# Layer 0's score maxima: two 64-row products per head pair instead of one product against a masked key operand

## What is computed

```
x = x + tanh(g_xattn[0]) * L0_xattn(layernorm(x), ctx)      # 16 heads of 64, 120 keys
x = x + tanh(g_ffn[0])   * L0_ffn(layernorm(x))             # 8 experts, weighted
x = x + tanh(g_xattn[1]) * L1_xattn(layernorm(x), ctx)      # 16 heads of 16, 120 keys
x = x + tanh(g_ffn[1])   * L1_ffn(layernorm(x))             # first 512 tokens

def L0_xattn(x, context):
    q, k, v = heads of x @ Wq.T, context @ Wk.T, context @ Wv.T
    sim = einsum('bihd,bjhd->bhij', q, k) * 64 ** -0.5
    attn = softmax(sim)                       # over the 120 keys
    return (attn @ v) @ Wo.T + bo
```

## Time and profile before

| | before |
|---|---|
| median of three runs | 3786.83 us (3785.24 to 3787.05) |
| the profiled execution's own time, its span | 3787.4 us |
| PE busy | 3715.2 us, 98% of the span |
| PE weight loads (PEld) busy | 2972.8 us, 78% |
| DVE busy | 2656.0 us, 70% |
| ScalarE (ACT) busy | 1751.9 us, 46% |
| POOL busy | 1382.3 us, 36% |
| one turn of the main loop | 56.50 us (layer 1's key product starts at 1800.51 us, the next batch's at 1857.01) |

### The profile page before, as it was taken

How to read it: one execution, slowest core, us unless ns; L and a number is a source line. 1 busy time by engine, 2 the same in 40 slices (tenths; PEclk the granted TensorE clock), 3 DMA queues, 4 the chain that set the end, 5 groups by cost and what they waited for, 6 DMA issues and landing times.

```text
span 3787.4 us, 96515 instructions
## 1 busy us (share of the span) xinstructions
PE 3715.2 (98%) x34836; PEld 2972.8 (78%) x34836; DVE 2656.0 (70%) x5694; ACT 1751.9 (46%) x3371; POOL 1382.3 (36%) x1333
## 2 busy tenths in 40 slices
PE   6999999999999999999999999999999999999998
PEld 5788788788788788878878878878878878878865
DVE  4676776776776776776776776777777777677675
ACT  4444445444445445445445445445444444444431
POOL 3334334334334334334334333333333333333323
PEclk9999999999999999999999999999999999999999
DMA  3000000000000000000000000000000000000011
GB/s 95 10 15 11 16 14 11 16 15 11 15 16 9 15 16 9 15 16 9 15 16 9 15 16 9 15 16 10 14 16 14 11 16 14 11 16 14 11 37 53
DMA packets 58915, 64.81 MB, mean 17 GB/s; under 512 B 5344, under 2 KB 55808, under 8 KB 58240
## 3 DMA queue, kind: packets, MB, share of 16 engines
q10 hardware_dynamic: 34688, 32.52, 2.8%
q1 hardware_dynamic: 24192, 31.81, 2.5%
HBM read 47.01 MB, written 17.30 MB: 17 GB/s over the span
## 4 chain that ended last, share of the span: by engine, by line
PE 84%; DVE 10%; issue 2%; POOL 1%; DVEq 1%; ACT 0%; POOLq 0%
PE g L821 25%; PE g L827 15%; PE scores L821 10%; PE scores L923 6%; PE g L981 6%; DVE xn L1179 4%; PE g L890 4%; PE g L990 3%; PE scores L974 3%; DVE y_nm L1257 3%; PE scores L955 3%; PE g L841 3%; PE scores L927 2%; PE g L901 1%; POOL y_rstd L543 1%
## 5 line engine op out<-in xcount | busy, mean ns | idle before, releaser
L760 ACT ACTIVATE prob<-scores 120x1024 f32<-120x1024 f32 x512 | 510.2, 1023 | 495.6 <-PE scores L927 324.5
L1318 DVE SCALAR_TENSOR_TENSOR x<-g,lg_w,x 128x256 f32<-128x256 f32 x1024 | 483.5, 482 | 59.6 <-PE g L821 32.2
L596 POOL TENSOR_TENSOR q_lo<-an,q_hi 128x512 fp32r<-128x512 f32 x256 | 329.5, 1287 | 345.0 <-ACT q_hi L793 345.0
L662 ACT CAST q_hi<-g 128x512 fp32r<-128x512 f32 x256 | 150.1, 586 | 579.1 <-PE g L821 579.1
L821 PE MATMUL g<-ew_hi,yT_hi 128*128 128x512 f32 x1024 | 412.0, 402 | 0.0
L541 POOL TENSOR_TENSOR y_rstd<-y_mv,eps 128x2 f32<-128x2 f32 x128 | 25.0, 195 | 1041.5 <-DVE y_mv L1174 1041.5
L821 PE MATMUL g<-ew_lo,yT_hi 128*128 128x512 f32 x1024 | 401.2, 392 | 0.0
L821 PE MATMUL g<-ew_hi,yT_lo 128*128 128x512 f32 x1024 | 399.7, 390 | 0.0
L1257 DVE TENSOR_REDUCE x_nm<-g 128x4 f32<-128x480 f32 x512 | 310.6, 649 | 104.8 <-PE g L890 104.8
L1257 DVE TENSOR_REDUCE y_nm<-g 128x4 f32<-128x480 f32 x512 | 301.1, 651 | 109.7 <-PE g L901 109.7
L591 POOL TENSOR_TENSOR q_lo<-q_full,q_hi 128x512 fp32r<-128x512 f32 x256 | 328.6, 1303 | 38.3 <-ACT q_full L694 38.0
(11 more groups left out here) (213 smaller groups left out, 9905.8 us busy)
## 6 DMA issues: line engine op xcount, KB each, us to landing
x_in<-in_x ACTq DMA_DIRECT2D x64, 256.0 KB, 2.9
out<-y_x SPq DMA_DIRECT2D x64, 256.0 KB, 2.1
ctx_in<-in_ctx ACTq DMA_DIRECT2D x128, 120.0 KB, 2.5
wk_s<-in_gu SPq DMA_DIRECT2D x8, 512.0 KB, 3.6
vx<-in_ew SPq DMA_DIRECT2D x2, 1024.0 KB, 5.1
wk_s<-in_wk SPq DMA_DIRECT2D x1, 1024.0 KB, 5.1
prob<-in_wq SPq DMA_DIRECT2D x1, 1024.0 KB, 7.8
wv_s<-in_wv SPq DMA_DIRECT2D x1, 1024.0 KB, 10.4
```

The costliest lines, as they stand in the source:

```text
L596: g.tensor_tensor(q[1][:, 2 * h:2 * h + 2, :], an[:, 2 * (h % 2):2 * (h % 2) + 2, :], q[0][:, 2 * h:2 * h + 2, :].bitcast(F32), ALU.subtra ...
L662: a.copy(dst, ring.bank(job)[:, 0:cols]).then_inc(done.sem, 1)
L760: a.activation(prob[:, e % 2].rearrange("p o u s -> p (o u s)"), scores[0:NK, banks, :].rearrange("p o c -> p (o c)"), ACT.Exp, scale=scal ...
L1318: ins = v.scalar_tensor_tensor(out=x1[:, t, :], in0=ring.bank(Y_FFN[j])[:, o * D:(o + 1) * D], scalar=lg_w[:, t, 2 * n + o:2 * n + o + 1], ...
```

## The change

`kmx`, its mask `half` with four small memsets, its semaphore `x_kmx` and POOL's function for the step `n_k` go. `x_max` on PE waits for the high part of the keys (`x_khi`) in place of `x_kmx`. Each pair is then multiplied by two matmuls: partitions 0 to 63 of `q` and `kT` give the first head of the pair, in the first of the step's two banks, and partitions 64 to 127 the second head, in the second bank. So a bank now holds one head of each of four pairs. Each matmul loads 64 x 128 weights and streams 120 columns. DVE's reductions have the same size, and write four adjacent values.

```
-            def x_k(i, c):
-                if first(i):
-                    pool.wait_ge(dve_zeroed, 1)
-                x_khi.wait(pool, i, 1 + c)
-                g.tensor_tensor(kmx[:, 4 * c:4 * c + 4, :, :],
-                                kT[0][:, 4 * c:4 * c + 4, :].bitcast(F32).unsqueeze(2).broadcast_to([P, 4, 2, NK]),
-                                half[:].unsqueeze(1).unsqueeze(3).broadcast_to([P, 4, 2, NK]),
-                                ALU.mult).then_inc(x_kmx.sem, 1)
...
             def x_max(i, n):
                 t, c = n // 2, n % 2
-                x_kmx.wait(pe, i, c + 1)
-                ring.to_fill(pe, i, X_MAX[2 * n:2 * n + 2], *X_Q[2 * c:2 * c + 2])
-                for job, pairs in zip(X_MAX[2 * n:2 * n + 2], ((0, 1), (2, 3))):
-                    for u in pairs:
-                        ins = t_.matmul(ring.bank(job)[:, u % 2 * 2 * NK:(u % 2 + 1) * 2 * NK],
-                                        q[0][:, 4 * c + u, t * P:(t + 1) * P], flat(kmx[:, 4 * c + u]), start=True, stop=True)
-                    ring.has_filled(ins, job)
+                x_khi.wait(pe, i, c + 1)
+                jobs = X_MAX[2 * n:2 * n + 2]
+                ring.to_fill(pe, i, jobs, *X_Q[2 * c:2 * c + 2])
+                for u in range(4):
+                    for o in range(2):
+                        rows = slice(64 * o, 64 * o + 64)
+                        ins = t_.matmul(ring.bank(jobs[o])[:, u * NK:(u + 1) * NK], q[0][rows, 4 * c + u, t * P:(t + 1) * P],
+                                        kT[0][rows, 4 * c + u, :], start=True, stop=True)
+                        if u == 3:
+                            ring.has_filled(ins, jobs[o])
...
-                by_pair = x_nm[:, t, :].rearrange("p (o k) -> p k o", o=2)
-                for j in range(2):
-                    maxima((i, X_MAX[2 * n + j]), by_pair[:, 4 * c + 2 * j:4 * c + 2 * j + 2, :])
+                for o in range(2):
+                    maxima((i, X_MAX[2 * n + o]), x_nm[:, t, 64 * o + 4 * c:64 * o + 4 * c + 4])
```

More of the change, by code:

```diff
@@ L298, in flamingo_stack @@
         kT = pair("kT", [P, NPAIR, NK])
-        kmx, half = sb("kmx", [P, NPAIR, 2, NK], F32R), sb("half", [P, 2])
         vx, ones = sb("vx", [P, INNER]), sb("ones", [P, 32])
@@ L347, in flamingo_stack @@
         x_hi, x_khi, x_qhi = signal("x_hi"), signal("x_khi", 2), signal("x_qhi", 4)
-        x_kmx, x_qlo = signal("x_kmx", 2), signal("x_qlo", 4)
+        x_qlo = signal("x_qlo", 4)
         x_scored, x_probs, x_mixed = (signal("x_scored", QUADS), signal("x_probs", QUADS),
@@ L627, in _ @@
             run(pool, {"n_stat": n_norm, "n_res": n_res, "p_stat": y_norm2, "y_stat3": y_stat3, "y_res": y_res, "y_k": y_k,
-                       "n_k": x_k, "n_q": x_q, "x_hi": x_lo, "m_zero": m_zero, "m_stat": m_stat, "m_sig": m_glu_up}, None, {AFTER_X[3]: ones1})
+                       "n_q": x_q, "x_hi": x_lo, "m_zero": m_zero, "m_stat": m_stat, "m_sig": m_glu_up}, None, {AFTER_X[3]: ones1})
         @block.scalar
@@ L1143, in _ @@
             v.memset(lg_w[:], 0.0)
-            for o in range(2):
-                for e in range(2):
-                    v.memset(half[64 * o:64 * o + 64, e:e + 1], float(o == e))
             for n in range(2):
```

## The result

The changed kernel takes 3851.01 us, the median of four runs (3847.4 to 3852.83), against 3786.94 us for the kernel before, measured beside it. The ratio is 1.0168, with a 95% interval of 1.0153 to 1.0182: 64 us or 1.7% slower. The profiled execution's span is 3848.6 us, 61.2 us over that of before.

What follows compares the result with a forecast made beforehand. PE, busy for 98% of the span, was taken to set the end. Shape changes less shorter last streams, with n_max 3 absorbed, gave 0.85 us per batch, 54 us over 64 batches: 3841 us, 1.4% slower, range 3808 to 3858.

Steps and rivals of the forecast that it cites:

- POOL's products are worth nothing: Dropping POOL's 128 masking products, 228.7 us, gains 0 to 0.9 us, taken as 0, since they were hidden.
- Term 1: Inside each n_max step, new pairs start 0.11 us apart, set by weight loads, as before; bounds 0.06 and 0.22.
- A: Half-height loads are faster, so pair distance follows the stream at 0.06 us: 26 us slower, 3812 us; chance 0.09.
- B: Shape change free between full-width weights and pairs 0.06 us apart: 38 us faster, 3749 us; chance 0.04.
- C: The two halves of a pair run one after the other: 83 to 115 us more, 3924 to 3956; chance 0.03.
- The shorter last stream, -0.05: In each n_max step the last pair streams half of the 240 columns, saving 0.05 us per step.
- Term 2: Each tile-shape change costs PE 0.20 us; n_max 0 and 2 add two each, n_max 1 and 3 one each.
- The unseen change from 32 to 64 rows: Going into n_max 1 and 3 from 32-row tiles, not in the trace: taken as 0.20 us, bounds 0 and 0.20.
- Term 3: The 0.15 us added by n_max 3 fits into PE's 0.24 us wait for DVE's transpose before the values product.
- The rival in which nothing is absorbed: n_max 3 is not absorbed: 1.00 us per batch, 64 us, 3851 us; inside the main case's 0.77 chance.
- The waits that could appear: Banks fill 0.16 to 0.2 us later, delaying DVE's reductions; taken as 0, at most 0.2 us per batch.
- The sum: n_max 0, 1 and 2 add 0.35, 0.15 and 0.35 us, n_max 3 absorbed: 0.85 us per batch, 54 us.

Runs made afterwards that it cites:

- e6: Changed kernel with kmx and half at their places and POOL's 128 masking products back, their result unread: 3836.44 us, ratio 1.0134.
- e1: Changed kernel with kmx and half still allocated but unused, so later tensors keep their old addresses: 3837.63 us, ratio 1.0116.
- e5: Changed kernel with three of each four 64-row matmuls streaming 240 columns instead of 120: 3850.40 us, ratio 1.0148.
- e2: Kernel before plus one 120-column matmul ahead of n_max 0, in two runs: 64 rows 3821.02 us, 128 rows (control) 3796.58 us.
- e4: Kernel before with n_max 0 alone in the new form, POOL's masks kept: 3809.84 us, ratio 1.0060.
- e3: Kernel before with n_max 3 alone in the new form, POOL's masks kept: 3789.23 us, ratio 0.9999.
- e7: Changed kernel with one unused 32-byte tensor where kmx and half were: 3838.28 us, ratio 1.0126.

## Why the prediction was right, point by point

- **What bounds the kernel.** Right. PE's busy time rose by 62 us and the span by 61.
- **POOL's products are worth nothing.** Right: e6 with them and e1 without them have the same turn.
- **Term 1, inner distance 0.11 by the loads.** Right, in the trace (0.11) and by e5, where twice the columns cost nothing. The Trainium skill's rule in "TensorE: Matmul & The Clock Gate", section "LDWEIGHTS (loading the stationary operand)", that rows do not shorten a load, holds here: the 128-row control in e2 adds 0.10 us and the 64-row pairs start 0.11 us apart. Rivals A, B and C fall with it. The "Up to 2×" of the Trainium skill, "TensorEngine Tiling (Array Packing)", section "Theoretical Speedup", does not come here: the pairs start 0.11 us apart, as the full-height products did.
- **The shorter last stream, -0.05.** Not shown as a term of its own. The way from the last pair to the gate product is still 0.20, and it is the first inner distance that is shorter, 0.16 instead of 0.21; e5 has 0.21 there again and the same 0.59 us for the step. So the 0.35 of `n_max` 0 came out, but as the price of two changes, 0.34 to 0.36 by e2 and e4, and not as 0.40 less 0.05. No run gives the last pair a wide stream.
- **Term 2, 0.20 us per shape change, six of them.** The mechanism and the count were right, the size slightly large where transposes follow. `n_max` 0 was put at 0.35 and is 0.34 (e4: 0.34). `n_max` 1 was put at 0.15 and is 0.10, `n_max` 2 at 0.35 and is 0.29: behind the change come transposes there, and the second of the pair at 1936.96 starts 0.44 - 0.27 = 0.17 behind the first, not 0.22. So the price of coming out is 0.06 us lower ahead of them. The unseen change from 32 to 64 rows costs what I took, within 0.03 us: 1936.14 to 1936.37.
- **Term 3, `n_max` 3 is absorbed.** Right, in the trace (0.90 and 0.91) and by e3. Counted as there, the value product could start at 1942.62 + 0.17 + 0.11 = 1942.90 and starts at 1942.94, and its load adds 0.11: the wait went from 0.24 to 0.15 us. The rival in which nothing is absorbed had 3851 us as its time, which is what was measured; the total alone would have spoken for it.
- **The waits that could appear** did not.
- **The sum.** 0.85 us per batch, 54 us in all. Measured without the shift of addresses: 0.67 per turn, and 49 us in all for e7 (3838.28 against 3788.92). That 0.67 is a difference of medians; the means of the 59 inner turns differ by 0.69, of which the four steps are 0.71. The expert products take 0.02 back: in the kernel before they lie between 226.7 and 228.1 ns a batch, in e1 nearly always at 226.7; why is open. Some 5 us more fall on the ends, where I had said within 1. The traces place them ahead of the loop: the first bias product starts at 92.1 us before, at 95.2 in the changed kernel, and at 96.4, 98.9 and 94.6 in e1, e7 and e6, which have the same steps on PE. The granted clock from 20 to 160 us is 0.91 before and 0.89, 0.92, 0.87 and 0.90 in these, so it can explain a part at most; the rest is open.
- **What was missing.** The prediction costed what the change takes out of the program and not that this moves the tensors behind it. That is worth 0.25 us per turn, 16 us. The steps came out some 10 us below the forecast (0.69 for 0.85) and the ends some 5 above, so the total was missed by 10 us only because errors cancelled, and it lay inside the range by the room that other cases had made. The forecast turn of 57.4 us was met (57.45) by the same luck. As a step it is the sentence "nothing moves" read too narrowly: no instruction moved, but `yT` did.

## What to carry to other kernels

Cutting a product into row tiles pays only if its stream, and not its weight load, sets the distance of starts; read both from the starts behind a shape change, where nothing was fetched ahead. Then count the changes of tile shape that a step adds with its neighbours in the order, at 0.10 to 0.18 us each by the runs here, since a tile step among full-height products pays twice and one behind another tile shape once. And when a change adds or drops an on-chip tensor, keep its place allocated in one comparison run, or an unrelated part of the kernel may answer for it.

## What was not expected of the hardware

- Where tensors start in SBUF changes the distance of back-to-back fp32r matmuls: 227 against 233 ns at 512 columns, 113.3 against 117.8 and 118.6 at 256, by moves of 32 to 96 bytes. That it is the stationary operand's own start is the likely reading, but each run moved other tensors too. The fastest expert products had `yT` and `ew` both at 128 within 256 bytes; the projections had theirs at 192 and 128. No single rule fits both.
- In the changed kernel the query projection runs at 116.8 ns instead of 117.8 although its own operands did not move. What else takes part in this is open.
- A matmul behind a shape change that streams 120 columns is followed by the next after 0.16 us, one that streams 240 after 0.21. The step as a whole takes 0.59 us with either, because the next change counts from the last weight load (0.25 to 0.26 us in e5 and the changed kernel).
